# Rounded query and key halves placed by DMA: a fused attention and MLP layer in float32 on one core

## The reference, cut to what matters

```
x = x + tanh(g_xattn) * wkv(w, u, layernorm(x), ctx)          # 4 batches, 512 x 512
h0 = layernorm(x)
n1, n2 = rmsnorm(h0, ln1_w), rmsnorm(h0, ln2_w)
q, k, v = (n1 @ W.T).reshape(b, 512, 16, 32)                   # 16 heads of 32
probs = softmax(causal(q @ k.T / sqrt(32)))                    # per head
attn = (probs @ v) @ Wo.T
mod = 0.1 * tanh(attn @ A)                                     # A: 512 x 16
gate = silu(n2 @ W_in.T + mod * (n2 @ A) @ B)
out = x + tanh(g_ffn) * (h0 + (gate * (n2 @ W_up.T)) @ W_down.T)
```

## Time and profile before

| what | us |
|---|---|
| device time, three runs | 1063.98, 1065.28, 1066.85 (median 1065.28) |
| profiled execution: span, first to last instruction | 1067.0 |
| PE busy | 946.0 (89%) |
| DVE busy | 641.0 (60%) |
| ACT busy | 412.6 (39%) |
| POOL busy | 343.2 (32%) |
| hardware DMA queue, share of 16 engines | 24.5% |

### The profile page before, as it was taken

The page is one execution under the profiler, slowest core; times in us unless marked ns, Lnnn a source line. Parts: engine busy times, 40 slices in busy tenths (PEclk is TensorE's granted clock), DMA queues, the critical chain, the costliest instruction groups (busy, mean ns, idle before and its releaser), DMA issues. The chain is left out here.

```text
span 1067.0 us, 13783 instructions
## 1 busy us (share of the span) xinstructions
PE 946.0 (89%) x4880; PEld 728.0 (68%) x4880; DVE 641.0 (60%) x1032; ACT 412.6 (39%) x725; POOL 343.2 (32%) x202
## 2 busy tenths in 40 slices
PE   3129999889899999898899999988899999999998
PEld 3127656777788766587688866677688875678886
DVE  7987653698456852678636864478835765232223
ACT  2406454222234555333233654333222555433331
POOL 7540011565440001365542001256544000254441
PEclk9559989899899989999899998999999998999999
DMA  9001213322222210522221220421222221122321
GB/s 280 32 1 40 47 35 112 107 63 85 90 89 72 61 41 2 188 79 70 89 81 49 81 66 18 150 97 60 89 78 78 72 52 41 50 89 94 102 80 42
DMA packets 33548, 81.37 MB, mean 76 GB/s; under 512 B 5648, under 2 KB 5648, under 8 KB 32400
## 3 DMA queue, kind: packets, MB, share of 16 engines
q1 hardware_dynamic: 33472, 80.41, 24.5%
HBM read 63.35 MB, written 4.19 MB: 63 GB/s over the span
## 5 line engine op out<-in xcount | busy, mean ns | idle before, releaser
L373 POOL TENSOR_TENSOR gu_lo<-raw_gu,gu_hi 128x1024 fp32r<-128x1024 f32 x64 | 153.2, 2394 | 589.4 <-ACT gu_hi L487 589.4
L913 PE MATMUL ps<-h_hi,gu_hi 128*128 128x512 f32 x512 | 205.6, 402 | 5.0 <-DVE gsil L867 5.0
L914 PE MATMUL ps<-h_lo,gu_hi 128*128 128x512 f32 x512 | 202.4, 395 | 0.0
L915 PE MATMUL ps<-h_hi,gu_lo 128*128 128x512 f32 x512 | 202.3, 395 | 0.0
L805 DVE TENSOR_REDUCE mx<-ps 128x1 f32<-128x512 f32 (+3 forms) x256 | 112.5, 484 | 74.3 <-PE ps L1006 73.6
L591 ACT ACTIVATE act_hi<-prod 128x512 fp32r<-128x512 f32 x64 | 40.4, 632 | 253.3 <-DVE prod L872 253.3
L867 DVE SCALAR_TENSOR_TENSOR gsil<-th,ps 128x512 f32<-128x512 f32 x64 | 43.3, 677 | 141.0 <-ACT th L587 141.0
L545 ACT ACTIVATE e_row<-ps 128x512 f32<-128x512 f32 (+1 forms) x192 | 90.8, 521 | 92.5 <-PE ps L1026 91.7
L377 POOL TENSOR_TENSOR wd_lo<-raw_d,wd_hi 128x512 fp32r<-128x512 f32 x64 | 94.1, 1470 | 90.4 <-ACT wd_hi L493 90.4
L913 PEld LDWEIGHTS ps<-h_hi,gu_hi 128*128 128x128 f32 x512 | 97.1, 190 | 30.2 <-DVE gsil L867 9.0
L915 PEld LDWEIGHTS ps<-h_hi,gu_lo 128*128 128x128 f32 x512 | 96.6, 189 | 22.7
(11 more groups left out here) (156 smaller groups left out, 1630.5 us busy)
## 6 DMA issues: line engine op xcount, KB each, us to landing
raw_gu<-w_gu_dram SPq DMA_DIRECT2D x64, 512.0 KB, 3.3
raw_d<-w_down_dram SPq DMA_DIRECT2D x64, 256.0 KB, 3.0
x_sb<-x_dram SPq DMA_DIRECT2D x16, 256.0 KB, 3.6
vT<-ctxT_dram SPq DMA_DIRECT2D x4, 1024.0 KB, 8.9
q_st<-q_st SPq DMA_DIRECT2D x16, 256.0 KB, 2.9
k_st<-k_st SPq DMA_DIRECT2D x16, 256.0 KB, 2.9
out_dram<-base SPq DMA_DIRECT2D x16, 256.0 KB, 2.1
q_st<-q_lo SPq DMA_DIRECT2D x32, 64.0 KB, 2.0
```

The costliest lines, as they stand in the source:

```text
L373: pool.tensor_tensor(gu_s[f % 2][1][:], raw_gu[f % 2][:], f32(gu_s[f % 2][0][:]), ALU.subtract).then_inc(gu_lo, 1)
L913: pe.matmul(dst, w_hi, m_hi, start=start, stop=False)
L914: pe.matmul(dst, w_hi, m_lo, start=False, stop=False)
L915: return pe.matmul(dst, w_lo, m_hi, start=False, stop=stop)
```

## The change

Groups 1 to 3 all take the staged path, and q and k have a staging tile each (`qk_hi4[0]`, `qk_hi4[1]`). ACT's `q_copy` and DVE's `k_copy` are gone: both hi copies of each head are now placed by DMA from the staging tile, 64 KB each. For q and for k that is 8 DMAs for hi and 4 for lo. ACT and DVE now wait for all 24 DMAs of the group before (`PLACED` = 24 x 16) before they overwrite the staging tiles. Group 0 keeps its old path. Apart from that, the values' tile `v_aug` is packed with 17 columns a head in place of 32.

```
-STAGED = 2
-ROUND_AT = (0, 2)
-LOW_HALF = (0, 1, 2, 3, 4, 5, 6, 7)
-STAGE_AT = {2: (5, 7), 3: (12, 14)}
-LOW_AT = {2: (6, 8), 3: (12, 14)}
-COPY_AT = {2: (5, 8), 3: (13, 15)}
+STAGE_AT = {1: (0, 2), 2: (5, 7), 3: (12, 14)}
+LOW_AT = {1: (0, 2), 2: (5, 7), 3: (12, 14)}
+PLACED = 384
...
-                        if g >= STAGED:
-                            sp.wait_ge(qk_lo, b * 2 * G + 2 * g + i + 1)
+                        if g == 0:
+                            sp.wait_ge(qk_hi, b * 8 + 4 * i + 4)
+                            sp.dma_start(f32(st[0][second:second + 32, :, :]), f32(st[0][0:32, :, :])).then_inc(rep_ld[0], 16)
+                        else:
+                            sp.wait_ge(qk_stage, b * 2 * (G - 1) + 2 * (g - 1) + i + 1)
                             if g >= 3:
                                 sp.wait_ge(st_ps, 2 * (b * STEPS + 6 * (g - 2)))
+                            for at in (0, second):
+                                for j in range(4):
+                                    sp.dma_start(f32(st[g % 3][at:at + 32, j, :]), f32(qk_hi4[i][quad(j), :])).then_inc(rep_ld[g], 16)
+                            sp.wait_ge(qk_lo, b * 2 * G + 2 * g + i + 1)
                             for j in range(4):
                                 sp.dma_start(f32(st[g % 3][low:low + 32, j, :]), f32(qk_lo4[i][quad(j), :])).then_inc(rep_ld[g], 16)
-                        sp.wait_ge(qk_hi, b * 8 * G + 8 * g + 4 * i + 4)
-                        sp.dma_start(f32(st[g % 3][second:second + 32, :, :]), f32(st[g % 3][0:32, :, :])).then_inc(rep_ld[g], 16)
...
                 def qk_stage_hi(g, i):
 
                     act.wait_ge(qk_ps, b * 2 * G + 2 * g + i + 1)
-                    act.wait_ge(qk_lo, b * 2 * G + 2 * g + i)
-                    act.wait_ge(qk_hi, b * 8 * G + 8 * g + 4 * i)
-                    act.activation(qk_hi4[:], ps[:, 4 + i, :], ACT.Copy).then_inc(qk_stage, 1)
+                    if g > 1:
+                        act.wait_ge(rep_ld[g - 1], PLACED * (b + 1))
+                    act.activation(qk_hi4[i][:], ps[:, 4 + i, :], ACT.Copy).then_inc(qk_stage, 1)
...
                 def qk_low4(g, i):
 
-                    dve.wait_ge(qk_stage, b * 2 * (G - STAGED) + 2 * (g - STAGED) + i + 1)
-                    if g > STAGED:
-                        dve.wait_ge(rep_ld[g - 1], 160 * (b + 1))
-                    dve.tensor_tensor(qk_lo4[i][:], ps[:, 4 + i, :], f32(qk_hi4[:]), ALU.subtract).then_inc(qk_lo, 1)
+                    dve.wait_ge(qk_stage, b * 2 * (G - 1) + 2 * (g - 1) + i + 1)
+                    if g > 1:
+                        dve.wait_ge(rep_ld[g - 1], PLACED * (b + 1))
+                    dve.tensor_tensor(qk_lo4[i][:], ps[:, 4 + i, :], f32(qk_hi4[i][:]), ALU.subtract).then_inc(qk_lo, 1)
...
-                        pe.wait_ge(rep_ld[g], (32 if g < STAGED else 160) * (b + 1))
+                        pe.wait_ge(rep_ld[g], (32 if g == 0 else PLACED) * (b + 1))
```

More of the change, by code:

```diff
@@ L28 @@
 G = H // 4
-VW = 32
+VW = R + 1
+VROW = H * VW + 16
 GA = H * R + R
@@ L123, in flamingo_layer @@
         b_s = place("b_s", [5 * R, FF], F32R)
-        v_aug = place("v_aug", [P, TB, H, VW], F32)
+        v_aug = place("v_aug", [P, TB, VROW], F32)
         k_st = [place(f"k_st{i}", [P, 4, T], F32R) for i in range(3)]
@@ L152, in flamingo_layer @@
         nmrow = place("nmrow", [8, T], F32R)
-        qk_hi4 = place("qk_hi4", [P, T], F32R)
+        qk_hi4 = [place(f"{n}_hi4", [P, T], F32R) for n in "qk"]
         qk_lo4 = [place(f"{n}_lo4", [P, T], F32R) for n in "qk"]
@@ L345, in _ @@
             pool.wait_ge(pool_own, 5)
-            pool.memset(v_aug[:, :, :, R:R + 1], 1.0).then_inc(const_rdy, 1)
+            for tb in range(TB):
+                op = pool.memset(v_aug[:, tb, 0:H * VW].rearrange("p (h r) -> p h r", r=VW)[:, :, R:VW], 1.0)
+            op.then_inc(const_rdy, 1)
             pool.memset(tcols[:], 0.0).then_inc(const_rdy, 1)
@@ L511, in qk_stage_hi, with qk_round @@
                     act.wait_ge(qk_ps, b * 2 * G + 2 * g + i + 1)
-                    act.wait_ge(qk_lo, b * 2 * G + 2 * g + i)
-                    act.wait_ge(qk_hi, b * 8 * G + 8 * g + 4 * i)
-                    act.activation(qk_hi4[:], ps[:, 4 + i, :], ACT.Copy).then_inc(qk_stage, 1)
-                def qk_round(g, i):
-                    act.wait_ge(qk_ps, b * 2 * G + 2 * g + i + 1)
-                    for j in range(4):
[L520 to L528, removed]
+                    if g > 1:
+                        act.wait_ge(rep_ld[g - 1], PLACED * (b + 1))
+                    act.activation(qk_hi4[i][:], ps[:, 4 + i, :], ACT.Copy).then_inc(qk_stage, 1)
+                def qk_round(i):
+                    act.wait_ge(qk_ps, b * 2 * G + i + 1)
+                    for j in range(4):
+                        act.activation((q_st, k_st)[i][0][0:32, j, :], ps[quad(j), 4 + i, :], ACT.Copy).then_inc(qk_hi, 1)
                 def values(tb):
@@ L532, in values @@
                     bank = VALUE_BANK[tb]
-                    act.activation(v_aug[:, tb, :, 0:R], ps[:, bank, 0:H * R].rearrange("p (h r) -> p h r", r=R), ACT.Copy)
+                    act.activation(v_aug[:, tb, 0:H * VW].rearrange("p (h r) -> p h r", r=VW)[:, :, 0:R], ps[:, bank, 0:H * R].rearrange("p (h r) -> p h r", r=R), ACT.Copy)
                     act.activation(h_a[:, tb, :], ps[:, bank, H * R:GA], ACT.Copy).then_inc(va_sb, 1)
@@ L552, in weighted @@
                     act.activation(pvs[:], ps[:, 6, :], ACT.Copy).then_inc(pvs_rdy, 1)
-                qk_round(0, 0)
-                qk_round(0, 1)
+                qk_round(0)
+                qk_round(1)
                 values(0)
@@ L565, in batch @@
                         exps(m)
-                    if n in ROUND_AT:
-                        qk_round(1, ROUND_AT.index(n))
                     for g, at in STAGE_AT.items():
@@ L570, in batch @@
                             qk_stage_hi(g, at.index(n))
-                    for g, at in COPY_AT.items():
-                        if n == at[0]:
-                            q_copy(g)
                     for tb, at in VALUE_AT.items():
@@ L770, in batch, with qk_low @@
                 own["base"], own["n"] = own_prologue + b * DVE_OWN_PER_BATCH, 0
-                def qk_low(g, i, heads=range(4)):
+                def qk_low(i):
                     st, at = ((q_st, 32), (k_st, 64))[i]
[L775 to L779, removed]
-                def qk_low4(g, i):
-                    dve.wait_ge(qk_stage, b * 2 * (G - STAGED) + 2 * (g - STAGED) + i + 1)
-                    if g > STAGED:
-                        dve.wait_ge(rep_ld[g - 1], 160 * (b + 1))
-                    dve.tensor_tensor(qk_lo4[i][:], ps[:, 4 + i, :], f32(qk_hi4[:]), ALU.subtract).then_inc(qk_lo, 1)
[L788 to L794, removed]
+                    for j in range(4):
+                        dve.wait_ge(qk_hi, b * 8 + 4 * i + j + 1)
+                        op = dve.tensor_tensor(st[0][at:at + 32, j, :], ps[quad(j), 4 + i, :], f32(st[0][0:32, j, :]), ALU.subtract)
+                    op.then_inc(qk_lo, 1)
+                def qk_low4(g, i):
+                    dve.wait_ge(qk_stage, b * 2 * (G - 1) + 2 * (g - 1) + i + 1)
+                    if g > 1:
+                        dve.wait_ge(rep_ld[g - 1], PLACED * (b + 1))
+                    dve.tensor_tensor(qk_lo4[i][:], ps[:, 4 + i, :], f32(qk_hi4[i][:]), ALU.subtract).then_inc(qk_lo, 1)
                 def maxima(n):
@@ L806, in maxima @@
                         op.then_inc(smax_rdy, 1)
-                        for c in range(8):
-                            if LOW_HALF[c] == 2 * n + i:
-                                qk_low(1, c // 4, (c % 4,))
                 def minus_max(g):
@@ L835, in weighted @@
                         dve.reduce_sum(modsum[:], terms, AX.X).then_inc(modsum_rdy, 1)
-                qk_low(0, 0)
-                qk_low(0, 1)
+                qk_low(0)
+                qk_low(1)
                 for n in range(STEPS + LAG):
@@ L846, in batch @@
                             qk_low4(g, at.index(n))
-                        if n == COPY_AT[g][1]:
-                            k_copy(g)
                     if n >= NORM_LAG and (n - NORM_LAG) % 6 == 0:
@@ L1050, in weigh @@
                         for j in range(4):
-                            op = pe.matmul(ps[quad(j), 6, kb * P:T], v_aug[:, kb, 4 * g + j, :], e_row[g % 2][:, j, E_AT[kb]:E_AT[kb] + w],
+                            op = pe.matmul(ps[quad(j), 6, kb * P:T], v_aug[:, kb, (4 * g + j) * VW:(4 * g + j) * VW + 32], e_row[g % 2][:, j, E_AT[kb]:E_AT[kb] + w],
                                            start=kb == 0, stop=kb == TB - 1)
```

## The result

The changed kernel takes 1134.3 us in the median of four runs (1130.6 to 1136.0), against 1065.65 us before: a ratio of 1.064, with a 95% interval of 1.061 to 1.067. It is 69 us slower, where 41 were forecast; 1134 lies above the range of 1093 to 1124. The profiled execution took 1135.9 us with a span of 1134.1; a run's time was 1.8 us above its span in every profiled run of this study, so the spans can be compared directly.

The account below looks back on a forecast made before the run. PE, busy 89% of the span, was taken as the bound; late DMA releases from SP's queue add 41.4 us to 1067.0, DVE's gain and the clock counting nothing: 1108.4 us span, 1106 us forecast, range 1093 to 1124.

Parts of the forecast that it names:

- the forecast's chain of fixed prices: Groups 1 to 3, last batch: scores(6) 2.4 us late, scores(12) 6.3, scores(18) 11.1; all batches 41.4 us.
- Twenty-four issues put the last start 14.3 us behind the first; 16.3 us to the release: SP's queue, each of groups 1 to 3: 23 pitches of 0.62 us, then 2.0 us to land.
- my row of four: SP's timeline before: four 64 KB DMAs of the added form, start 864.55, next one 867.04, read as 0.62 us each.
- I take nothing for the sum: PE's granted clock around scores(12) and scores(18): counted as zero, with -7 and +22 us kept for the range.
- the first: Rival 1, scores(12) to scores_T(5) wholly at 1.2 GHz: 22 us more, 1128 us; chance 12%.
- the second: Rival 2, both waits end with most of the low clock time over: 7 us less, 1099 us; chance 12%.
- a row in the MLP: PE idle 4.2 us there: clock fell inside the idle time, stayed low the next 5.2 us, then full again.
- That early batches add 1.5 us less: The two early batches, 1.5 us slower before, lose 9.6 us each where the two late ones lose 11.1.
- Behind `scores(18)` nothing changes: After scores(18): maxima(2)'s DMAs follow stack(3) within 2 us, needed two steps later; no further delay, MLP unaffected.
- DVE's relief is swallowed: DVE's 7.4 us less a batch could give back at most 3.0 us; PE just waits longer at scores(12) and scores(18).
- Rival 3: SP's pitch up to 0.41 us: copies stay hidden, DVE's relief counts, kernel faster at 1057 us; chance 4%.
- The rules weighed: SP's issues: skill page's small dispatch time would hide 24 issues (1.2 us); its coalescing rule and the trace say otherwise.

Follow-up runs that it names:

- e6: The changed kernel with unread matmuls on PE in the two long waits (18 ahead of scores(12), 24 ahead of scores(18)): 1118.2 us, ratio 1.049.
- e1: The kernel before with v_aug packed and nothing else changed: 1065.0 us, ratio 1.000.
- e7: The changed kernel with the 12 copies of each group's keys issued by POOL, SP issuing only the queries' 12: 1062.0 us, ratio 0.996.
- e5: The changed kernel with the second hi copy as one 256 KB DMA out of the first, 18 issues a group instead of 24: 1105.3 us, ratio 1.039.
- e4: The kernel before, v_aug packed, with 48 added DMAs of 2 KB a batch on SP into a tile nobody reads: 1142.4 us, ratio 1.072.
- e9: The changed kernel with the staging of group 2's queries one step later, behind nmrow in ACT's order: 1126.6 us, ratio 1.055.
- e3: Against the kernel before, group 1 staged too, but hi copies stay on ACT and DVE, 10 issues a group: 1065.8 us, ratio 1.001.
- e8: The changed kernel with the keys' 12 copies of each group issued by ACT behind their staging: 1121.9 us, ratio 1.052.
- e11: The kernel before with four unread matmuls ahead of each of maxima_T(2) and maxima_T(3): 1054.5 us, ratio 0.989.

## Why the prediction was wrong

The mechanism stood, on every link; the size did not. Two terms of the sum failed: the release of a group, put 0.9 us too short, and the clock, put at nothing. By the prediction's own steps, with the distances from `scores(0)` to `scores(18)` on PE's timeline in the four batches: before 48.1, 48.1, 46.8 and 46.6 us; 57.7 in each by the forecast's chain of fixed prices (41.1 us more in all; the forecast took 11.1 for the third batch too, so 41.4); measured 63.5, 62.4, 63.3 and 61.9.

- **"Twenty-four issues put the last start 14.3 us behind the first; 16.3 us to the release": this term was too short by 0.9 us a group.** Measured from SP's first issue to the start of `scores` in the first batch: 17.5, 17.9 and 17.4 us; in the last 17.4, 16.6 and 16.6; on average over twelve groups 17.2. That is 11.0 of the missing 28 us. The pitch was nearly right: the four groups without a long issue need 14.5 to 14.6 us for 23 steps, 0.63 each with the hand-overs between tiles, and 16.6 to 16.8 to `scores`. What was not in my row of four is one issue in each of the other eight groups (all three of the first batch) that takes 1.0 to 1.5 us. It shows as 3.31 us for four in SP's timeline above, where the next four take 2.49.
- **"I take nothing for the sum" for the clock: this is the step whose reasoning failed.** I had the price of a low stretch between `scores(12)` and `scores_T(5)` as 1.8 to 5.5 us, and set it off against a saving behind `scores(18)`. The first came true, near its lower end (7.4, 7.7, 8.3 and 8.1 us where 5.5 stood: 9.5 us over the four batches), the second did not: behind `scores(18)` the low level lasts 11.8 us in the last batch, though it had fallen 5 us before the wait's end, and the stretch to `gate_mod` is 0 to 1 us longer than before, not 3.5 shorter. So neither rival came about: not the first, with 5.5 us a batch at `scores(12)`, and not the second, with a net gain. I read the recovery from a row in the MLP, with other matmuls behind it. The nearer row was the earlier trace rows, the same stretch of the same kernel, and it had some 10 us of it (a mean of 0.53 over 11). e6 shows the clock's share by taking it away: 16 us come back. That is not all loss of the change: of the 10.2 us that e6 wins behind `scores(18)` the change had added only 2.3, and the kernel before pays the rest too.
- **That early batches add 1.5 us less, since the chain hangs on fixed prices: about right.** Their `scores(18)` came at the same distance as in the late ones, within 1.6 us, whatever it had been before. But the 1.5 us were no property of early batches: there the trace before has a stretch of 3.4 us at the low level between `scores(6)` and `scores(12)` (118.6 to 122.0 us, mean clock 0.50), and in e1's trace all four batches take 46.7 to 46.9 us.
- **Behind `scores(18)` nothing changes: nearly.** With 2.3 us there and 3.4 us in the prologue and from `gate_mod` to the next batch, the sum is 41.1 + 20.2 + 2.3 + 3.4 = 67.0 us, with 20.2 the excess of the measured distances over the forecast ones; the spans differ by 67.1. For the 3.4 us I have no cause. They are no more than two executions of nearly the same kernel differ by: e1's trace has 1.7 us more than the one before in the prologue and 2.1 less from `gate_mod` on. The trace of e7 is longer than the one before by 1.3 to 2.4 us from `gate_mod` to the next `scores(0)` in each of the first three batches. That stays open.
- **DVE's relief is swallowed: right in the change** (its 2.1 us of waits fall to 0.3, and PE waits for DMAs instead). Where the DMAs are hidden, in e7, `scores(18)` comes 1.7 to 3.0 us sooner than in the trace before (1.8 sooner than in e1's), against up to 3.0 in the forecast.
- **Rival 3 did not come about, but its reasoning held.** Its condition, a pitch of 0.41 us on one queue, failed by 0.2 us. e7 halves the queue instead, and its outcome appears: all but 0.7 us hidden, and faster than before.
- **The rules weighed.** The Trainium skill's sentence ("DMA: Bandwidth & Descriptors", "Issuing engines are not separate DMA queues") that issuing from several engines saves only the sequencer's time holds as far as e7 shows it (the same 24 copies and bytes, and only SP has fewer issues); but that this time is "usually small relative to the DMA itself" does not hold here: 24 x 0.62 = 14.9 us against 2.0 us to land, and saving it by a second queue was worth 72 us (e7). Its rule to coalesce small transfers held (e5).

The two terms together, 10.95 and 9.5 us, less 0.2 for the steps between, are the 20.2 above. Shown by experiment: the count of issues on SP, whatever they carry (e4, e5, e7), the clock's share (e6), the link through `nmrow` (e9), and that staging and packing are free (e1, e3). Only argued: the cause of the one long issue in a group. All eight of them in the change overlap a packet of 0.9 to 1.2 us on the queue that loads instructions, and none of SP's 320 other issues into `q_st` and `k_st` takes over 0.70 us. e4 has eight as well, six of them DMAs of 2 KB, each beside such a packet, so the bytes of the copies do not make them. No run takes these packets away.

## What to carry to other kernels

Before work moves from a compute engine to DMAs, multiply the issues by the pitch of a like row on the issuing queue, and lay that beside the time until someone waits: bytes and landing time may be the smaller part. Look for a second queue whose engine is idle before giving the plan up. And price every new wait of PE of some microseconds with the low clock behind it, from the row of the same stretch, not from another stage's.

## What the runs showed of the hardware

- SP needs 0.62 us for a DMA of 64 KB in 32 rows and for one of 2 KB in 32 rows alike (e4); for the former ACT needs 0.64 us (e8: 5.11 for eight) and POOL 0.50 (e7). The copies landed 2.0 us behind SP's issue.
- The granted clock fell from 2.4 to 1.2 GHz behind short waits too: in the kernel before, two waits of 0.6 and 0.9 us within 4 us end in some 10 us at the low level. Four matmuls of 128x512 in the second of them kept it full in this stretch (e11).
- The low level's length differed by stretch: about 5 us of it behind an idle time of 4.2 us in an MLP, 11.8 us behind one of 6.0 us at `scores(18)`.
